# Adapter product and mixture of experts: the first batch's h comes back from DRAM and is turned on VectorE

## What is computed

```
h = einsum('bsi,boi->bso', x, weight[adapter_ids])      # 8 x 256 x 1024
logits = h @ gate_w.T;  probs = softmax(logits);  top 2, normalized
expert e:  (silu(h @ Wg_e.T) * (h @ Wu_e.T)) @ Wd_e.T
shared:    (silu(h @ Sg.T) * (h @ Su.T)) @ Sd.T
out = x + sum over top 2 of weight * expert + shared
```

## Time and profile before

| | |
|---|---|
| median of 3 runs | 1081.92 us |
| the profiled execution: time | 1081.02 us |
| its span in the trace | 1079.5 us |
| TensorE busy | 1068.7 us (99%) |
| VectorE busy | 618.2 us (57%) |
| ScalarE busy | 476.3 us (44%) |
| DMA, mean over the span | 223 GB/s |

### The profile page before, as it was taken

How to read it: one execution, slowest core, us unless ns; L and a number is a source line. 1 busy time by engine, 2 the same in 40 slices (tenths; PEclk the granted TensorE clock), 3 DMA queues, 4 the chain that set the end, 5 groups by cost and what they waited for, 6 DMA issues and landing times.

```text
span 1079.5 us, 15991 instructions
## 1 busy us (share of the span) xinstructions
PE 1068.7 (99%) x4938; PEld 881.8 (82%) x4939; DVE 618.2 (57%) x650; ACT 476.3 (44%) x569; POOL 285.0 (26%) x325
## 2 busy tenths in 40 slices
PE   8999999999999999999999999999999999999998
PEld 7888888888888888888888887878888888888887
DVE  6655555436675668686866767345562545534454
ACT  6656565533222467665755755333222322222310
POOL 1000000000005666556655660221003110032040
PEclk9999999999999999999999999999999999999999
DMA  9766665632245778998897876473466435563355
GB/s 350 298 251 251 235 241 189 223 145 79 78 195 205 262 264 277 354 320 299 306 359 263 299 247 240 163 291 131 82 246 242 170 117 140 231 233 136 117 184 206
DMA packets 46389, 240.66 MB, mean 223 GB/s; under 512 B 6354, under 2 KB 12626, under 8 KB 36434
## 3 DMA queue, kind: packets, MB, share of 16 engines
q1 hardware_dynamic: 20434, 154.15, 39.3%
q0 software_dynamic: 19008, 62.41, 16.8%
q10 hardware_dynamic: 6912, 23.66, 5.7%
HBM read 200.87 MB, written 43.52 MB: 226 GB/s over the span
## 4 chain that ended last, share of the span: by engine, by line
PE 97%; DMA 1%; issue 1%; ACT 1%; DVE 0%; ACTq 0%; SPq 0%; DVEq 0%
PE bank L526 31%; PE bank L528 31%; PE bank L527 31%; PE bank L547 1%; PE bank L539 1%; PE bank L733 1%; DMA raw<-cond_w 1%; ACT w_split_sb L804 0%; DVE w_split_sb L1067 0%; PE bank L667 0%; PE bank L556 0%; DMA ids<-ids 0%; ACT y_out L804 0%; PE bank L654 0%; PE bank L699 0%
## 5 line engine op out<-in xcount | busy, mean ns | idle before, releaser
L1067 DVE TENSOR_TENSOR w_split_sb<-raw,w_split_sb 128x2048 fp32r<-128x2048 f32 (+3 forms) x152 | 258.7, 1724 | 86.4 <-ACT w_split_sb L804 86.1
L804 ACT ACTIVATE w_split_sb<-raw 128x2048 fp32r<-128x2048 f32 (+3 forms) x152 | 218.3, 1461 | 72.1 <-PE bank L528 53.8
L465 POOL DMA_INDIRECT h_in<-h_dram,idx_h x156 | 186.2, 1193 | 114.4 <-DVE tile_f L1351 68.1
L526 PE MATMUL bank<-hT_hi,w_split_sb 128*128 128x512 f32 x512 | 199.8, 390 | 0.6 <-DVE w_split_sb L1067 0.6
L528 PE MATMUL bank<-hT_hi,w_split_sb 128*128 128x512 f32 x512 | 199.2, 389 | 0.0
L527 PE MATMUL bank<-hT_lo,w_split_sb 128*128 128x512 f32 x512 | 199.2, 389 | 0.0
L526 PE MATMUL bank<-w_split_sb,tile_hT 128*128 (+1 forms) x312 | 124.8, 400 | 1.4 <-issue 1.4
L528 PE MATMUL bank<-w_split_sb,tile_hT 128*128 (+1 forms) x312 | 122.0, 391 | 0.0
L527 PE MATMUL bank<-w_split_sb,tile_hT 128*128 (+1 forms) x312 | 121.7, 390 | 0.0
L526 PEld LDWEIGHTS bank<-hT_hi,w_split_sb 128*128 128x128 f32 x512 | 96.1, 188 | 20.7 <-issue 0.9
L528 PEld LDWEIGHTS bank<-hT_hi,w_split_sb 128*128 128x128 f32 x512 | 96.1, 188 | 20.2
(11 more groups left out here) (152 smaller groups left out, 1466.0 us busy)
## 6 DMA issues: line engine op xcount, KB each, us to landing
raw<-sh_gu_w SPq DMA_DIRECT2D x16, 2048.0 KB, 9.0
raw<-exp_gu_w SPq DMA_DIRECT2D x16, 2048.0 KB
raw<-cond_w SPq DMA_DIRECT2D x14, 2048.0 KB, 8.5
y_dram<-y_out ACTq DMA_DIRECT2D x39, 512.0 KB, 4.1
raw<-sh_down_w SPq DMA_DIRECT2D x8, 2048.0 KB, 7.7
raw<-exp_down_w SPq DMA_DIRECT2D x16, 1024.0 KB, 9.2
h_dram<-h_blk POOLq DMA_DIRECT2D x16, 512.0 KB, 6.3
x_raw_sb<-xT SPq DMA_DIRECT2D x7, 1024.0 KB, 9.5
```

The source lines that it names most:

```text
L465: nc.gpsimd.indirect_dma_start(out=h_in[par][:, i, :], out_offset=None, in_=h_blocks, in_offset=bass.IndirectOffsetOnAxis(ap=idx_h[par][:, ...
L526: nc.tensor.matmul(dst, lhs[0], rhs[0], start=first, stop=False)
L804: return nc.scalar.activation(dst, src, ACT.Copy)
L1067: return nc.vector.tensor_tensor(dst, src, hi.bitcast(F32), ALU.subtract)
```

## The change

A second way for h to become `hT` exists already, in the shared stage; the change uses it in the cond stage for half of the tokens of quarters 0, 1 and 2. The quarter 3 (`DQ`) is done as before.

- TensorE doesn't transpose units 0 to 3 of quarters 0 to 2, and ScalarE doesn't copy them to `h_row`; `turned_units` counts the units that are still transposed.
- POOL loads the first batch's h back from `h_dram` to a new tile `c_blk`, four loads of 256 KB in rows of 1 KB, ahead of the second batch's stores. It waits for both stores of the first batch, and for the turning of the quarter before.
- In unit 0 of the next quarter VectorE turns `c_blk` into `q_f32` with two transposes of 128x1024; in unit 1 ScalarE makes the high part (two copies of 128x1024) and VectorE the low part.
- The router stands behind the matmuls of unit 2 instead of unit 1, and waits for that low part; VectorE takes its result in unit 2; the logits are transposed back after unit 4 instead of unit 3.
- In quarter 3 the high and low parts of `hT` of units 0 and 1 are both made in unit 2, since the router before reads that part of `hT` until then.
- Quarter 3 is written out on TensorE, and quarters 0 and 3 on POOL; the loops run over the others. Some waits of the later stages have other counts.

```diff
--- before.py
+++ after.py
@@ -107,6 +107,7 @@
     h_blk = at("h_blk", [P, 2, BLOCKS, KT, 32], F32, 192)
     q_blk = at("q_blk", [P, QTOK // 32, HID // BLOCKS], F32, 144)
     q_f32 = at("q_f32", [P, KT, QTOK], F32, 176)
+    c_blk = at("c_blk", [P, SEQ // 32, HID // BLOCKS], F32, 118)
     h_in = [at(f"h_in{i}", [P, BLOCKS, HID // BLOCKS], F32, 192 + 4 * i) for i in range(2)]
 
     rt = {}
@@ -196,6 +197,7 @@
         lg_ev = sem("lg_ev")
         h_store = [sem(f"h_store{i}") for i in range(2)]
         hT_in = [sem(f"hT_in{j}") for j in range(BLOCKS)]
+        batch_in = [sem(f"batch_in{j}") for j in range(BLOCKS)]
         hT_turned = sem("hT_turned")
         hT_hi = sem("hT_hi")
         hT_split = sem("hT_split")
@@ -278,6 +280,15 @@
                                  h_quarters[bass.ds(qq, 1), j, :, :, :].rearrange("o t i c -> (o t) i c")).then_inc(hT_in[j], 16)
 
         UPQ = 2 * QM
+        DQ = QUARTERS - 1
+
+        def turned_units(q, u):
+
+            return DQ * UPQ // 2 + u if isinstance(q, int) and q == DQ else UPQ // 2 * q + u - UPQ // 2
+
+        def has_turn(q, u):
+            return isinstance(q, int) and q == DQ or u >= UPQ // 2
+
         LAST_S = TILES - 1
         POST = COND_CHUNKS + SH_CHUNKS
 
@@ -425,16 +436,27 @@
             nc.gpsimd.iota(small["pcol"][:, :], pattern=[[0, 1]], base=0, channel_multiplier=1,
                            allow_small_or_imprecise_dtypes=True).then_inc(consts, 1)
 
-            def cond_stores(q):
+            def cond_stores(q, first=False, last=False):
 
                 for b2 in range(2):
+                    if b2 == 1 and not last:
+                        for m in range(2):
+                            wait(h_store[m], 16 * (2 * q + 1))
+                        if not first:
+                            wait(hT_turned, 2 * q)
+                        for j in range(BLOCKS):
+                            pool.dma_start(c_blk[32 * j:32 * (j + 1), :, :],
+                                           h_batches[bass.ds(2 * q, 1), j, :, :, :].rearrange("o t i c -> (o t) i c")).then_inc(batch_in[j], 16)
                     for m in range(2):
                         wait(hb_ev, UPQ * q + 4 * b2 + 2 + m + 3)
                         pool.dma_start(h_dram[bass.ds(q * QTOK + b2 * SEQ + m * P, P), :],
                                        h_blk[:, m, :, :, :].rearrange("p j k c -> p (j k c)")).then_inc(h_store[m], 16)
 
-            with pool.Fori(0, QUARTERS) as q:
+            h_batches = h_dram.rearrange("(b i t) (j c) -> b j t i c", b=BATCHES, t=32, j=BLOCKS)
+            cond_stores(0, first=True)
+            with pool.Fori(1, DQ) as q:
                 cond_stores(q)
+            cond_stores(DQ, last=True)
 
             def store_rows(src, dst, row0, count, which=range(QM)):
 
@@ -533,15 +555,17 @@
 
             def transpose_unit(q, u):
                 m = u % 2
-                pe.wait_ge(h_ev, UPQ * q + u + 3)
-                pe.wait_ge(t_lo, UPQ * q + u + 1)
+                pe.wait_ge(h_ev, turned_units(q, u) + 3)
+                pe.wait_ge(t_lo, turned_units(q, u) + 1)
                 for i in range(4):
                     last = nc.tensor.transpose(bank[4 + m][:, i * P:(i + 1) * P], h_row[:, m, i * P:(i + 1) * P], ident[:, :])
                 last.then_inc(t_mm, 1)
 
             def router(q):
 
-                pe.wait_ge(t_lo, UPQ * q + UPQ + 2)
+                pe.wait_ge(t_lo, turned_units(q, UPQ - 1) + 3)
+                if not (isinstance(q, int) and q == DQ):
+                    pe.wait_ge(hT_split, 2 * q + 2)
                 for k in range(KT):
                     for hl in range(2):
                         last = nc.tensor.matmul(bank[6][:, :], gate_pair[:, k, :], hT[hl][:, k, :],
@@ -581,13 +605,13 @@
                                                [x_split_sb[b2][:, hl, k, m * P:(m + 1) * P] for hl in range(2)],
                                                w_cols(n, k, 0, HALF), k == 0, k == KT - 1)
                             last.then_inc(h_mm, 1)
-                            if u == 1 and not first:
+                            if u == 2 and not first:
                                 router(q - 1)
-                            if u:
+                            if u and has_turn(q, u - 1):
                                 transpose_unit(q, u - 1)
-                            elif not first:
+                            elif u == 0 and not first:
                                 transpose_unit(q - 1, UPQ - 1)
-                            if u == 3 and not first:
+                            if u == 4 and not first:
                                 transpose_logits(q - 1)
 
 
@@ -598,8 +622,9 @@
             pe.wait_ge(consts, 1)
             cond_quarter(0, first=True)
             pe.wait_ge(gate_lo_done, 1)
-            with pe.Fori(1, QUARTERS) as q:
+            with pe.Fori(1, DQ) as q:
                 cond_quarter(q)
+            cond_quarter(DQ)
 
 
             def shared_half(half, c, par, fb, between=None):
@@ -681,7 +706,7 @@
             first_inner(0, 0)
             transpose_unit(QUARTERS - 1, UPQ - 1)
             first_inner(1, 0)
-            pe.wait_ge(t_lo, UPQ * QUARTERS + 2)
+            pe.wait_ge(t_lo, turned_units(DQ, UPQ - 1) + 3)
             first_inner(0, KT // 2).then_inc(sg_mm, 1)
             first_inner(1, KT // 2).then_inc(su_mm, 1)
             router(QUARTERS - 1)
...
@@ -833,7 +858,7 @@
             def unit_hi(q, u, first=False):
                 b2, n, m = u // 4, u // 2 % 2, u % 2
                 t0 = b2 * SEQ + m * P
-                act.wait_ge(t_mm, UPQ * q + u + 3)
+                act.wait_ge(t_mm, turned_units(q, u) + 3)
                 if not first:
                     act.wait_ge(lg_mm, q)
                 copy(hT[0][:, 4 * n:4 * n + 4, t0:t0 + P], bank[4 + m][:, :].rearrange("p (k t) -> p k t", k=4)).then_inc(t_hi, 1)
@@ -859,16 +884,24 @@
                         act.wait_ge(h_mm, UPQ * q + 4 * b2 + 2)
                         x_hi_part(2 * q + b2 + 1, 1 - b2)
                     act.wait_ge(h_mm, UPQ * q + u + 3)
-                    act.wait_ge(t_mm, UPQ * q + u + 1)
-                    copy(h_row[:, m, :], bank[m][:, :]).then_inc(h_ev, 1)
+                    if has_turn(q, u):
+                        act.wait_ge(t_mm, turned_units(q, u) + 1)
+                        copy(h_row[:, m, :], bank[m][:, :]).then_inc(h_ev, 1)
                     if n == 0 and (not first or b2):
                         act.wait_ge(h_store[m], 16 * (2 * q + b2))
                     copy(h_blk[:, m, :, 4 * n:4 * n + 4, :].rearrange("p j k c -> p k j c"),
                          bank[m][:, :].rearrange("p (k j c) -> p k j c", k=4, j=BLOCKS)).then_inc(hb_ev, 1)
-                    if u:
+                    if last and u in (1, 2):
+                        for v in range(u) if u == 2 else ():
+                            unit_hi(q, v, first)
+                    elif u and has_turn(q, u - 1):
                         unit_hi(q, u - 1, first)
-                    elif not first:
+                    elif u == 0 and not first:
                         unit_hi(q - 1, UPQ - 1, second)
+                    if u == 1 and not first:
+                        for h in range(2):
+                            act.wait_ge(hT_turned, 2 * q + h - 1)
+                            copy(hT[0][:, 4 * h:4 * h + 4, 0:SEQ], q_f32[:, 4 * h:4 * h + 4, 0:SEQ]).then_inc(hT_hi, 1)
 
             cond_quarter(0, first=True)
             cond_quarter(1, second=True)
...
@@ -1101,7 +1134,7 @@
             def unit_lo(q, u):
                 b2, n, m = u // 4, u // 2 % 2, u % 2
                 t0 = b2 * SEQ + m * P
-                dve.wait_ge(t_hi, UPQ * q + u + 1)
+                dve.wait_ge(t_hi, turned_units(q, u) + 1)
                 lo(hT[1][:, 4 * n:4 * n + 4, t0:t0 + P], bank[4 + m][:, :].rearrange("p (k t) -> p k t", k=4),
                    hT[0][:, 4 * n:4 * n + 4, t0:t0 + P]).then_inc(t_lo, 1)
 
@@ -1128,13 +1161,27 @@
                         w_lo_half(4 * q + 2 * b2 + n + 1, (n + 1) % 2, m)
                     if n == 0 and m == (first and u < 2) and not (last and b2 == 1):
                         x_lo_part(2 * q + b2 + 1, 1 - b2)
+                    if u == 2 and not first:
+                        logits_T_out(q - 1)
+                    if last and u in (1, 2):
+                        for v in range(u) if u == 2 else ():
+                            unit_lo(q, v)
+                    elif u and has_turn(q, u - 1):
+                        unit_lo(q, u - 1)
+                    elif u == 0 and not first:
+                        unit_lo(q - 1, UPQ - 1)
                     if u == 1 and not first:
-                        logits_T_out(q - 1)
-                    if u:
-                        unit_lo(q, u - 1)
-                    elif not first:
-                        unit_lo(q - 1, UPQ - 1)
-                    if u == 3 and not first:
+                        for h in range(2):
```

(10 more changed lines are left out.)

14 lines of the change are left out of this document (7 added, 7 removed).

## The result

The kernel after took **1086.68 us** (median of 6 runs, 1085.02 to 1088.27), the kernel before 1081.64 beside it (6 runs, 1081.17 to 1082.76): a ratio of 1.0045 [1.0032, 1.0058]. I had forecast 1081.0, 0.9 faster, in a range of 1077.8 to 1084.0: it came out 5.0 slower. The profiled execution took 1087.66 us.

What follows compares the result with a forecast made beforehand. TensorE was taken as the bound (97% of the chain). 5.8 us of removed transposes less waits of 0.5, 1.5, 1.5 and 1.1 and 0.25 gave 0.9 us faster: 1081.0 us from the median 1081.92, range 1077.8 to 1084.0.

Steps and rivals of the forecast that it cites:

- The price of a transposed unit, 0.48: TensorE, cond stage: each transposed unit costs 5.92 - 5.44 = 0.48 us; 12 removed in quarters 0 to 2 save 5.8 us.
- The turn, the deciding term: VectorE, unit 0 of quarters 1 to 3: the two 128x1024 transposes take 2.37 us, as in the shared stage.
- The waits at unit 2: TensorE waits there for the weight split, delayed by the turn: 1.5, 1.5 and 1.1 us in quarters 1, 2, 3.
- The router waits for nothing: Moved behind unit 2, the router finds hT's low part ready about 177.1, before TensorE arrives at 179.4: no cost.
- Quarter 3: Cond stage: it keeps its transposes and gets the wait at unit 2, so it is 1.1 us slower.
- Quarter 0: Cond stage: no turned batch there, transposes of three units gone before unit 4; 1.4 us gained.
- the wait at its unit 4: TensorE in quarter 0 arrives at 32.65 but the late weight split lets unit 4 start at 33.15: 0.5 us.
- Rival (b): TensorE does not wait at unit 2, all 5.8 us kept: 1076.2, or 1078.5 for half; chance 0.21.
- I take nothing: POOL's queue: the four loads, 1 MB in 1 KB rows, take 4.5 us and are charged no time.
- the weight load with its 4.9 us to spare: Weight load issued at 148.7, landing at 157.3, read by ScalarE at 162.23; the loads could delay it.
- its own length plus 0.08: TensorE: the first matmul after a wait takes about 0.08 us more of pitch, 0.25 for three waits.
- Rival (c): The loads make unit 5's weight load over 4.9 us late, lengthening the waits at unit 2: 1087.0; chance 0.10.

Runs made afterwards that it cites:

- e17: The after kernel with run-time bounds, VectorE's turn behind the second split half, and the four loads on ScalarE's queue behind unit 5: 1078.43 us, ratio 0.9975.
- b0: The before kernel with run-time bounds on the numbers the expert stage loads: 1083.86 us, ratio 1.0025 to before.
- e4: The after kernel with run-time bounds and the four loads behind the second batch's first store on POOL's queue: 1082.99 us.
- e8: The after kernel with bounds, the four loads as one 1 MB load over 128 partitions in 8 KB rows, data order changed: waits at unit 2 1.28, 1.28, 0.76 us.
- e14: Like e8, one 1 MB load over 128 partitions, but in rows of 1 KB: waits at unit 2 1.28, 1.28, 0.76 us.
- c0: The after kernel with run-time bounds on the numbers the expert stage loads: 1087.09 us, ratio 1.0058 to before.
- e3: The after kernel with bounds, c_blk loaded in quarter 0 only, later quarters turning the old block: waits at unit 2 3.70, 1.28, 0.77 us.
- e7: The after kernel with bounds, four loads still onto 32 partitions each but in 8 KB rows, data order changed: waits at unit 2 3.06, 2.71, 0.76 us.
- e16: The after kernel with bounds, four 256 KB loads onto 128 partitions each in 2 KB rows, data order changed: waits at unit 2 1.29, 1.28, 0.77 us.
- e18: e8 plus an unused VectorE reduction (128x2048) behind the turn, to lengthen the wait: waits at unit 2 3.48, 3.47, 2.95 us.
- e19: e8 plus an unused VectorE reduction of half size (128x1024) behind the turn: waits at unit 2 2.41, 2.40, 1.89 us.
- e2: The after kernel with bounds and 20 small unused matmuls on TensorE behind unit 1 of quarters 1 to 3: 1086.59 us.
- e1: The after kernel with bounds and VectorE's turn moved to unit 1, behind the second half of the weight split: 1081.03 us, ratio 0.9991.
- e5: The after kernel with bounds and the edits of both e1 and e4: 1079.84 us, ratio 0.9983.

## Why the prediction was wrong, point by point

- **The price of a transposed unit, 0.48, held**: units without transposes are 5.44 long, and e17's quarters are together 5.3 us shorter than before's (its median is 5.4 below b0's).
- **The turn, the deciding term, held**: 2.36 for the pair, against 2.37 in the earlier trace rows. The Trainium skill (VectorE: DVE Perf Modes, "The three transpose paths") gives 311 ns for a 128x128 tile in bf16. My estimate from it, 2.5 us for an instruction of eight such tiles, does not hold for this one in float32: it takes 1.18.
- **The waits at unit 2**, forecast 1.5, 1.5, 1.1, are 1.28, 1.28 and 0.76 where no transfer is late (e4, e8, e14). The two are counted differently: the brackets count from the end of the last matmul, the forecast from when the next could have started. So counted, from start to start, e4 has 1.44 or 1.45 twice and 1.0: the order on VectorE was priced rightly. The router waits for nothing in after, as said. Quarter 3 came at +1.00, forecast +1.1. Quarter 0, forecast 1.4 shorter, is 1.5 shorter in c0 and 0.5 in after, whose first unit lost 1.5 to the clock; the wait at its unit 4, forecast 0.5, is 0.28 in c0 and absent in after. Rival (b) had a wait of zero at unit 2: only moving the turn gives it.
- **The step that failed is the DMA part, "I take nothing".** I costed the loads by their own landing, at 4.5 us (from the first issue to the last landing they took 15.2, 17.3 and 10.6), and looked at one neighbour, the weight load with its 4.9 us to spare. I did not look at the load of x, issued right behind them and read by the first link of the chain to unit 2, nor at the stores that free `h_blk`. In after they took 16.1 and 11.75 us; in e4, with the same loads behind the next store, neither was late for TensorE's chain. In before the load of x of the stretch that I took as the pattern landed at 159.09 and was read at 164.03: 4.9 us to spare, no more than the weight load had. Sized: the waits of quarters 1 and 2 are 1.7 and 1.1 above 1.28.
- **The term that was missing is the clock**: 1.7 us behind each wait of 2.37 and 2.99, 3.5 together. I had priced a wait as its own length plus 0.08; e4's waits cost 0.13, and these 1.7.
- Together, for quarters 1 and 2: from start to start the waits are 3.15 and 2.54, 2.7 more than the forecast's 3.0; the long units are 3.5, less the 0.16 that I had priced, 3.3. That makes 6.0, and between the forecast (51.3 each) and the trace lie 6.0. Quarter 0 adds 0.9.
- **Rival (c)** had the right kind, late transfers through the same chain, at 1087.0, but the wrong transfer, and got 0.10: I had judged it by the bytes of 1 MB, and the windows show that narrow loads also take throughput from the rest. That its number lies 0.3 from the result is luck, since it has neither the clock nor these transfers.

Shown: that the loads make the excess and that their place decides it (e3, e4), that their width does, as long as there are no more than four (e7 against e8, e14, e16), that a longer wait alone brings the low clock (e18, e19). Not settled: how 32 partitions at a time lower the throughput, and how much ScalarE's queue does. Open: the eight wide loads, the five longer executions of e2, and what besides its length decides whether a wait of about 2 us costs clock.

## What to carry over

A new transfer is to be held against every transfer of its stretch that a chain to the bottleneck reads, the stores that free a buffer among them, and not only against the one with the least known slack. Work added to an in-order engine belongs behind what the bottleneck waits for: here the same three turns, one split half later, were worth 6.1 us with the loads where after has them (e1 against c0) and 3.2 with the loads later (e5 against e4). A wait of TensorE of about 2 us or more may cost its length and 1.7 us again; so a forecast has to ask of each wait whether it stays below that.
